# First norms of groups 2 to 7 in period 0, a token-order router, and the experts' input split on GpSimd

## The chip, the core and the metric

The kernel runs on one core of one Trainium2 chip. The metric is the device time of one execution in microseconds (us), the median of several runs. The five engines of the core each follow an instruction list of their own and meet at semaphores: TensorE (PE in the profile), VectorE (DVE), ScalarE (ACT), GpSimd (POOL), and SyncE (SP), which issues most of the transfers.

## The reference

The input `x` is (16, 64, 16, 16) in fp32: 16 images, 64 channels, 256 positions. Three blocks add to it: a graph convolution behind a group norm, a selective state-space layer behind a layer norm over the 64 channels of a token, and a mixture of eight experts, two per token, behind a second such norm.

```python
x = x + L0_conv(_gn(x), ...)
t = _to_tokens(x)                    # 16 x 256 tokens of 64 channels
t = t + L1_attn(_ln_t(t), ...)       # "first norm": x_proj = norm(t) @ W_in
t = t + L1_ffn(_ln_t(t), ...)        # "second norm": router and experts read it
# in L1_attn: a scan over time, for 128 inner channels x 16 states
h_new = exp(dt * A) * h + dt * B * x_t;   y_t = (h_new * C).sum(-1)
# in L1_ffn, xt being _ln_t(t):
logits = xt @ Wr + br;   weights of the two largest of softmax(logits)
xn = (xt - mu) * rsqrt(var + eps)    # a norm of the normed input
h = gelu((xn * ln_g + ln_b) @ W1 + b1);   y = h @ W2 + b2
```

## The kernel before, in words

Channels lie on the partitions, two images side by side (64 + 64 partitions), so a **group** is two images and there are eight, 0 to 7, each 128 x 256 numbers. The state-space layer sees a group as 128 inner channels x 512 tokens. A prepared stage does the convolution and leaves its result in `res`; then `body` runs on every engine for **periods** i = 0 to 7. In period i the scan of group i runs; the experts of group i-1 (`prev`) are worked out beside it, and the first norm, projections and step sizes of group i+2 (`nxt2`) and the broadcast transfers of group i+1 (`nxt`) are made ready. Period 0 has no experts. After period 7 comes a tail: the experts of group 7 alone.

The order on each engine is written out by hand; nothing is scheduled. Main parts of one period:

- **VectorE**: eight slots (`dve_slot`, L797), each a product into PSUM (L810) and a scan of 1024 columns (L816). After slot 0: `dve_gate` (L833, gates the last period's scan output), `dve_relu`, `dve_t1` (adds the residual). After slot 1: the second norm's products and the router. That is `dve_lnF` (L844, `tns`), four half-width products with the experts' input in `dve_xn2` (L849: `xnt2` in fp32 and `X2`'s upper half, rounded to fp32r), two router steps in between (`dve_router1`), then eleven small ones (`dve_router2`, L872) with the first norm's product for group i+2 (`dve_xn`, L819) inside. Later, four products with the experts' outputs (`dve_mes`).
- **ScalarE**: sixteen decays (`act_decay`, L602, exp of 128 x 510; blocks 8 to 15 read PSUM that TensorE fills just before, `pe_spread`), between them the squares, Ln and Exp of the two norms (`act_lnF1`, `act_lnF2`, `act_lnA1`, `act_lnA2`), one Exp for the router, 16 gelus, three table loads, and copies.
- **GpSimd**: eight products of the scans with C (`pool_slot`, L348), the step sizes of the next group (`step_input`), the low part of the experts' input (`pool_x2`, L391: fp32 minus rounded, 64 x 512), the router's last five small steps (`pool_router`, L399), sums of the expert outputs.
- **TensorE**: the spreads, the norms' centring and averaging as matrix products with `cen_m` and `avg_m`, the router's logits (`pe_router`), the experts. Each first layer is two products, with high and low weights, on `X2`, which holds the rounded input on partitions 0 to 63 and the remainder on 64 to 127. Behind four first layers `pe_wt` (L1230) transposes the token weights that `pool_router` made, then second and first layers alternate to the end. Then the projections of group i+2 and `pe_sum` (L1107), the sums over states, whose last quarter waits for GpSimd's slot 7 and releases the next `dve_gate`. `pe_warm` are products whose result nobody reads.

In period 0 ScalarE itself issues the transfers of group 1's step sizes (`step_out`, L710).

## Time and profile before

| | |
|---|---|
| median of 3 runs | 395.13 us (391.87 to 396.75) |
| profiled execution | 391.73 us, span 390.0 us |
| busy: PE, DVE | 327.2 us (84%), 322.9 us (83%) |
| busy: ACT, POOL | 277.1 us (71%), 267.6 us (69%) |
| mean granted TensorE clock | 0.948 of full speed |

Busy shares are means over a preparation of about 55 us, eight periods and a tail of 35 us. In the periods VectorE, ScalarE and TensorE are all close to full, so a share alone doesn't tell which of them ends a period; the timelines of one period do. Period i is taken from one gate on VectorE to the next. The "granted clock" is the share of TensorE's full clock that the chip let through: 1.0 is 2.4 GHz, 0.5 is 1.2 GHz.

### The profile page before, as it was taken

The page shows a single profiled execution, that of the slowest core. Times are in us where ns is not written, and L with a number is a line of the kernel's source. Part 1 is how long each engine was busy: PE and PEld are TensorE (multiplying, and loading weights), DVE is VectorE, ACT ScalarE, POOL GpSimd, SP SyncE. Part 2 cuts the span into 40 slices and gives each one's busy share as a digit, 9 for nine tenths or more (in the row PEclk, how much of TensorE's full clock was granted, in tenths as well). Part 3 has the DMA queues.
Part 4 walks back from the last instruction along what each step waited for, and adds up shares of the span by engine and source line. Part 5 has one row for each costly group of instructions (what it writes and reads, how often), then busy time and mean ns, then how long its engine had stood idle before and what let it go on. Part 6 is the DMA issues. An engine that isn't in the chain of part 4 may idle for free. (4 is left out here: it accounts for less than half of the span.)

```text
span 390.0 us, 5520 instructions
## 1 busy us (share of the span) xinstructions
PE 327.2 (84%) x1680; PEld 178.4 (46%) x1680; DVE 322.9 (83%) x428; ACT 277.1 (71%) x465; POOL 267.6 (69%) x255
## 2 busy tenths in 40 slices
PE   0597897488899889978997899799889877998894
PEld 0475445232555345434544453455245424545452
DVE  2774466997999999999999999999999989994411
ACT  1003557589988997899789979997998749661472
POOL 8804403797669967996699589958985895692132
PEclk9996999558999999999999999999999998999698
...
GB/s 192 226 109 59 2 145 229 213 221 224 208 214 225 221 194 221 182 135 230 197 181 135 226 198 195 125 213 229 180 134 212 228 162 8 2 3 13 0 2 13
DMA packets 21301, 59.54 MB, mean 153 GB/s; under 512 B 4988, under 2 KB 13336, under 8 KB 15384
## 3 DMA queue, kind: packets, MB, share of 16 engines
...
q8 instruction: 14, 0.23, 0.3%
q14 instruction: 15, 0.12, 0.1%
...
## 5 line engine op out<-in xcount | busy, mean ns | idle before, releaser
L353 POOL TENSOR_TENSOR hs<-hs,Cs 128x1024 f32<-128x1024 f32 x63 | 149.6, 2377 | 39.5 <-DVE hs L816 38.8
L816 DVE TENSOR_TENSOR_SCAN hs<-av,P 128x1024 f32<-128x1024 f32 x64 | 146.3, 2286 | 4.8 <-ACT av L617 1.5
L680 ACT ACTIVATE hb<-P,b1c 128x512 f32<-128x512 f32 x128 | 81.3, 686 | 12.2 <-PE P L1266 11.9
L810 DVE TENSOR_TENSOR P<-P,ub 128x1024 f32<-128x1024 f32 x62 | 76.0, 1225 | 2.3 <-DMA ub<-u_scratch 0.6
L1280 PE MATMUL P<-hb,W2s 128*64 128x256 f32 x512 | 69.5, 395 | 0.0
L1265 PE MATMUL P<-X,W1H 128*128 128x512 f32 x128 | 57.8, 451 | 4.2 <-ACT hb L680 3.2
L1266 PE MATMUL P<-X,W1L 128*128 128x512 f32 x128 | 52.4, 409 | 0.0
L617 ACT ACTIVATE av<-P,Aneg 128x510 f32<-128x510 f32 x68 | 43.9, 685 | 9.8 <-PE P L1209 6.2
L1280 PEld LDWEIGHTS P<-hb,W2s 128*64 128x64 f32 x512 | 31.6, 137 | 31.0 <-issue 21.2
L617 ACT ACTIVATE av<-av,Aneg 128x510 f32<-128x510 f32 x60 | 38.2, 707 | 0.1
L1209 PE MATMUL P<-D,selD 128*128 128x512 f32 x64 | 29.8, 507 | 6.8 <-ACT av L617 4.2
L1265 PEld LDWEIGHTS P<-X,W1H 128*128 128x128 f32 x128 | 24.8, 194 | 22.5 <-ACT hb L680 15.0
L1117 PE MATMUL P<-hs,selS 128*32 128x512 f32 x256 | 30.6, 598 | 3.9 <-POOL hs L353 3.9
L673 ACT ACTIVATE wbs<-P 128x512 f32<-128x512 f32 x32 | 19.1, 598 | 15.4 <-PE P L1245 15.4
L367 POOL TENSOR_TENSOR accs<-accs,mes 128x512 f32<-128x512 f32 x21 | 26.9, 1282 | 2.4 <-DVE mes L917 2.4
L1266 PEld LDWEIGHTS P<-X,W1L 128*128 128x128 f32 x128 | 25.1, 196 | 3.8 <-issue 1.0
L1209 PEld LDWEIGHTS P<-D,selD 128*128 128x128 f32 x64 | 12.3, 198 | 19.3 <-issue 18.0
L917 DVE TENSOR_TENSOR mes<-P,wbs 128x512 f32<-128x512 f32 x28 | 18.6, 666 | 0.0
L1117 PEld LDWEIGHTS P<-hs,selS 128*32 128x32 f32 x256 | 6.8, 109 | 25.9 <-POOL hs L353 13.7
L907 DVE SCALAR_TENSOR_TENSOR mes<-P,cols,wbs 128x256 f32<-128x256 f32 x8 | 3.5, 480 | 16.5 <-PE P L1280 8.8
L1296 PE MATMUL P<-W1H 128*128 128x512 f32 x53 | 16.0, 406 | 0.0
L389 POOL TENSOR_TENSOR D<-dts,D 64x512 fp32r<-64x512 f32 x8 | 10.2, 1271 | 7.8 <-ACT D L600 6.9
...
## 6 DMA issues: line engine op xcount, KB each, us to landing
...
```

The costliest lines, as they stand in the source:

```text
L353: gp.tensor_tensor(hs[:, at, :, :], hs[:, at, :, :], rep(Cs[:, p, :], 1, 2), ALU.mult).then_inc(S["cm"], 1)
L367: done = gp.tensor_tensor(acc[:, :, :], prev, mes[:, at:at + 2, :], ALU.add)
L617: a_.activation(steps, dt_of, ACT.Exp, scale=Aneg[:, m:m + 1]).then_inc(S["aexp"], 1)
L673: a_.activation(wbs[:, 2 * r:2 * r + 2, :].rearrange("p e f -> p (e f)"), P[:, YS, :], ACT.Copy).then_inc(S["wb"], 1)
L680: a_.activation(hb[:, r % 4, :], P[:, (XA, XB)[r % 2], :], ACT.Gelu, bias=b1c[:, r:r + 1]).then_inc(S["gl"], 1)
L810: v.tensor_tensor(ring, rep(P[:, BB, :], 1, 2), ub[:, 2 * n:2 * n + 2, :], ALU.mult).then_inc(S["bm"], 1)
L816: v.tensor_tensor_scan(hs[:, (SLOTS * g + n) % RING].rearrange("p a t -> p (a t)"), av[:, 2 * n:2 * n + 2, :].rearrange("p a t -> p (a t)" ...
L1117: last = pe.matmul(P[32 * q:32 * q + 32, YS, :], selS[:, k, :], hs[:, (SLOTS * g + n) % RING, q % 2, :], start=(k == 0), stop=(k == 3))
L1209: pe.matmul(P[:, (YS, XA)[m % 2], :], selD[:, m - BY_PE[0], :], D2[:, :], start=True, stop=True).then_inc(S["dt_pe"], 1)
L1265: pe.matmul(P[:, bank, :], W1H[:, e, 128 * k:128 * k + 128], X2[:, :], start=True, stop=False)
L1266: pe.matmul(P[:, bank, :], W1L[:, e, 128 * k:128 * k + 128], X2[:, :], start=False, stop=True).then_inc(S["f1"], 1)
L1280: last = pe.matmul(P[64 * h:64 * h + 64, (XC, XD)[pair % 2], HW * (e % 2):HW * (e % 2) + HW], W2s[:, e, k, :], hb[:, r % 4, HW * h:HW * h ...
```

## The change

Three things are done, and order is moved around them.

1. **First norms in period 0.** Groups 2 to 7 get their first norm in period 0 already, two groups at a time (512 columns): `pe_cenP`, `act_lnP1`, `pe_varP`, `act_lnP2`, `dve_xnp`, k = 0, 1, 2. The results stay on chip in `xnl` (128 x 6 x 256). The per-period norm of group i+2 goes from all engines in periods 0 to 5.
2. **Token-order router.** The logits are now made from `t1` itself, with router weights that were multiplied by `cen_m` once (`Wrc`). The variance is made once more with tokens on the partitions (`pe_vartok`: 128 x 4), so ScalarE's Ln and Exp for the router shrink from 128 x 256 to 128 x 4. VectorE scales 128 x 32 logits and adds the bias, in place of the product `tns` of 128 x 256. Four of the router's results go to PSUM that lay in SBUF before.
3. **Experts' input.** VectorE makes one product of 128 x 256 (`dve_xn1`) where it made four of 64 x 256. GpSimd rounds it (two casts of 64 x 256) and takes the remainder (two subtractions of 64 x 256), before its product of slot 1 from period 1 on. In period 0 slot 1 goes ahead of `step_input`.

Buffers are laid over others to make room. In the tail the experts' input is made on VectorE as before, the router's logits move ahead, and the idle products are 2, 3 and 9 where they were 2, 4, 6 and 3.

```diff
+        sq2, rqs = hb[:, 3, 0:HW], hb[:, 3, HW:T]
+        sq, rs = ygs[:, 0:HW], ygs[:, HW:T]
+        sqp = mes[:, 0:2, :].rearrange("p r t -> p (r t)")
+        rsp = mes[:, 2:4, :].rearrange("p r t -> p (r t)")
...
         def pool_x2(eng, g):
...
             eng.wait_ge(S["xn2"], 2 * (g + 1))
-            eng.wait_ge(S["xh2"], 2 * (g + 1))
-            eng.wait_ge(S["cm"], min(SLOTS * (g + 1) + 2, SLOTS * G))
-            since(eng, "acc", EXP * g)
-            gp.tensor_tensor(X2[64:128, :], xnt2[:, :], X2[0:64, :], ALU.subtract).then_inc(S["xl2"], 1)
+            since(eng, "f1", EXP * KC * g)
+            eng.wait_ge(S["u"], so_far(g, 3))
+            eng.wait_ge(S["cm"], SLOTS * (g + 1) + 1)
+            for h in range(2):
+                q = slice(64 * h, 64 * h + 64)
+                gp.tensor_copy(X2[q, HW * h:HW * h + HW], xn[q, :]).then_inc(S["xh2"], 1)
+            for h in range(2):
+                q, o = slice(64 * h, 64 * h + 64), slice(64 - 64 * h, 128 - 64 * h)
+                eng.wait_ge(S["xh2"], 2 * g + h + 1)
+                low = gp.tensor_tensor(X2[o, HW * h:HW * h + HW], xn[q, :], X2[q, HW * h:HW * h + HW], ALU.subtract)
+            low.then_inc(S["xl2"], 1)
...
+                if i == 0:
+                    pool_slot(eng, i, p, 1)
                 if nxt is not None:
                     step_input(eng, gp, nxt, q)
-                pool_slot(eng, i, p, 1)
                 if prev is not None:
                     pool_x2(eng, prev)
+                    eng.wait_ge(S["xl2"], prev + 1)
+                if i > 0:
+                    pool_slot(eng, i, p, 1)
+                if prev is not None:
                     pool_router(eng, prev)
...
+        def act_lnP1(eng, k):
+            eng.wait_ge(S["cen1"], k + 3)
+            since(eng, "var1", k + 2)
+            a_.activation(sqp, P[:, XD, :], ACT.Square).then_inc(S["sq1"], 1)
+
+        def act_lnP2(eng, k):
+            eng.wait_ge(S["var1"], k + 3)
+            eng.wait_ge(S["xn1"], 2 * k + 2)
+            a_.activation(rsp, P[:, XC, :], ACT.Ln, bias=epst[:, 0:1]).then_inc(S["ln1"], 1)
+            eng.wait_ge(S["ln1"], k + 3)
+            a_.activation(rsp, rsp, ACT.Exp, scale=-0.5).then_inc(S["rs1"], 1)
...
         def act_rs2(eng, g):
-            a_.activation(rs2[:, :], P[:, XB, HW:T], ACT.Ln, bias=epst[:, 0:1]).then_inc(S["ln2"], 1)
+            eng.wait_ge(S["vt"], g + 1)
+            a_.activation(rv[:, 6], P[:, XC, 4 * EXP:4 * EXP + 4], ACT.Ln, bias=epst[:, 0:1]).then_inc(S["ln2"], 1)
...
         def act_lnF2(eng, g):
...
+            act_rq(eng, g)
+            act_rs2(eng, g)
+            act_rq_exp(eng, g)
+            act_rs2_exp(eng, g)
...
+                if i == 0:
+                    act_lnP1(eng, 0)
                 act_decay(eng, i, *((4, 5, 6, 7) if i > 0 else (6, 7)))
                 if i == 0:
+                    act_lnP2(eng, 0)
...
@@ -716,17 +739,20 @@
...
                 act_decay(eng, i, 11)
-                if nxt2 is not None:
-                    act_lnA1(eng, nxt2)
-                act_decay(eng, i, 12, 13)
+                if i == 0:
+                    act_lnP1(eng, 1)
+                act_decay(eng, i, 12)
+                if i == 0:
+                    act_lnP2(eng, 1)
                 if prev is not None:
                     act_router(eng, prev)
-                if nxt2 is not None:
-                    act_lnA2(eng, nxt2)
+                act_decay(eng, i, 13)
...
                     act_dhi(eng, nxt)
+                    act_lnP1(eng, 2)
                     act_c(eng, nxt, q, YS)
+                    act_lnP2(eng, 2)
...
+        def dve_xnp(eng, k):
+            eng.wait_ge(S["rs1"], k + 3)
+            if k == 2:
+                eng.wait_ge(S["g_mm"], 2)
+            v.tensor_tensor(xnl[:, 2 * k:2 * k + 2, :].rearrange("p g f -> p (g f)"), P[:, XD, :], rsp, ALU.mult).then_inc(S["xn1"], 2)
...
+        def dve_xn1(eng, g):
+            eng.wait_ge(S["rq"], g + 1)
+            since(eng, "xl2", g)
+            v.tensor_tensor(xn, P[:, XB, 0:HW], rqs, ALU.mult).then_inc(S["xn2"], 2)
...
         def dve_router1(eng, g):
-            logits = P[:, XC, 0:4 * EXP].rearrange("p (c e) -> p c e", e=EXP)
-            eng.wait_ge(S["lg"], 2 * (g + 1))
+            logits = P[:, XC, 224:224 + 4 * EXP].rearrange("p (c e) -> p c e", e=EXP)
+            eng.wait_ge(S["rs2"], g + 1)
+            eng.wait_ge(S["lg"], g + 1)
+            scaled = P[:, XC, 192:192 + 4 * EXP].rearrange("p (c e) -> p c e", e=EXP)
+            v.tensor_tensor(scaled, P[:, XC, 0:4 * EXP].rearrange("p (c e) -> p c e", e=EXP), rep(rv[:, 7], 2, EXP), ALU.mult).then_inc(S["lm"], 1)
+            eng.wait_ge(S["lm"], 2 * g + 1)
+            v.tensor_tensor(logits, scaled, rep(brs[:, :], 1, 4), ALU.add).then_inc(S["lm"], 1)
+            eng.wait_ge(S["lm"], 2 * g + 2)
             v.tensor_reduce(rv[:, 0], logits, AX, ALU.max).then_inc(S["m1"], 1)
...
-            v.scalar_tensor_tensor(out=rt[:, 5], in0=rt[:, 4], scalar=-2.0, in1=chances, op0=ALU.mult, op1=ALU.add).then_inc(S["e2"], 1)
+            v.scalar_tensor_tensor(out=left, in0=rt[:, 4], scalar=-2.0, in1=chances, op0=ALU.mult, op1=ALU.add).then_inc(S["e2"], 1)
...
-            v.tensor_tensor(rt[:, 6], rt[:, 5], bc(2), ALU.is_equal).then_inc(S["s2"], 1)
+            v.tensor_tensor(second, left, bc(2), ALU.is_equal).then_inc(S["s2"], 1)
...
-            v.tensor_tensor(rt[:, 7], rt[:, 6], rank[:, :, :], ALU.mult).then_inc(S["s2r"], 1)
+            v.tensor_tensor(weighed, second, rank[:, :, :], ALU.mult).then_inc(S["s2r"], 1)
...
                 if prev is not None:
-                    dve_lnF(eng, prev)
-                    dve_xn2(eng, prev)
-                    dve_router2(eng, prev, nxt2)
+                    dve_router1(eng, prev)
+                    dve_xn1(eng, prev)
+                    dve_router2(eng, prev)
...
                 dve_slot(eng, i, 3)
+                if i == 0:
+                    dve_xnp(eng, 0)
                 dve_slot(eng, i, 4)
                 experts(0)
                 dve_slot(eng, i, 5)
                 if i == 0:
-                    dve_xn(eng, 2)
+                    dve_xnp(eng, 1)
                 experts(2)
                 dve_slot(eng, i, 6)
+                if i == 0:
+                    dve_xnp(eng, 2)
...
+        def pe_cenP(eng, k):
+            eng.wait_ge(S["xn1"], 2 * k + 2)
+            pe.matmul(P[:, XD, :], cen_m[:, :], res[:, slice(2 * (k + 1) * HW, 2 * (k + 2) * HW)], start=True, stop=True).then_inc(S["cen1"], 1)
+
+        def pe_varP(eng, k):
+            eng.wait_ge(S["sq1"], k + 3)
+            eng.wait_ge(S["sg"], 2)
+            since(eng, "ln1", k + 2)
+            pe.matmul(P[:, XC, :], avg_m[:, :], sqp, start=True, stop=True).then_inc(S["var1"], 1)
...
         def pe_router(eng, g):
             eng.wait_ge(S["t1"], g + 1)
-            pe.matmul(P[:, XC, 0:4 * EXP], ident[:, :], rep(brs[:, :], 1, 4), start=True, stop=False).then_inc(S["lgb"], 1)
-            eng.wait_ge(S["tn"], g + 1)
+            eng.wait_ge(S["wrc"], 1)
             for q in range(2):
-                pe.matmul(P[:, XC, 2 * EXP * q:2 * EXP * q + 2 * EXP], tns[:, 128 * q:128 * q + 128],
-                          Wrt[:, :, :].rearrange("p h e -> p (h e)"), start=False, stop=(q == 1)).then_inc(S["lg"], 1)
+                last = pe.matmul(P[:, XC, 2 * EXP * q:2 * EXP * q + 2 * EXP], t1[:, 2 * (g % 2), 128 * q:128 * q + 128],
+                                 Wrc[:, :, :].rearrange("p h e -> p (h e)"), start=True, stop=True)
+            last.then_inc(S["lg"], 1)
+
+        def pe_vartok(eng, g):
+            eng.wait_ge(S["sq2"], g + 1)
+            for q in range(2):
+                last = pe.matmul(P[:, XC, 4 * EXP + 2 * q:4 * EXP + 2 * q + 2], sq2[:, 128 * q:128 * q + 128],
+                                 avg_m[:, 0:128:64], start=True, stop=True)
+            last.then_inc(S["vt"], 1)
...
             pe_dtz(eng, 1)
+            pe_cenP(eng, 0)
...
+            eng.wait_ge(S["ld_dup"], 64)
+            last = pe.matmul(P[:, XB, 2 * EXP * 2:2 * EXP * 2 + 2 * EXP], cen_m[:, :], Wrt[:, :, :].rearrange("p h e -> p (h e)"), start=True, stop=True)
...
                 pe_spread(eng, i, 9)
+                if i == 0:
+                    pe_varP(eng, 0)
...
-                    eng.wait_ge(S["xn1"], so_far(prev, 3))
+                    eng.wait_ge(S["xn1"], G)
                     since(eng, "me", EXP * prev)
+                    pe_router(eng, prev)
                     pe_warm(eng, 2, XD)
                     pe_varF(eng, prev)
+                    pe_vartok(eng, prev)
                 pe_spread(eng, i, 11)
                 pe_spread(eng, i, 12)
-                if nxt2 is not None:
-                    pe_cenA(eng, nxt2)
-                if prev is not None:
-                    pe_router(eng, prev)
+                if i == 0:
+                    pe_cenP(eng, 1)
                 pe_spread(eng, i, 13)
-                if nxt2 is not None:
-                    pe_varA(eng, nxt2)
+                if i == 0:
+                    pe_varP(eng, 1)
                 pe_spread(eng, i, 14)
                 pe_spread(eng, i, 15)
                 if prev is not None:
-                    eng.wait_ge(S["xh2"], 2 * (prev + 1))
+                    eng.wait_ge(S["xn2"], 2 * (prev + 1))
                     pe_warm(eng, 2, XB)
+                if i == 0:
+                    pe_cenP(eng, 2)
                 if nxt is not None:
                     pe_c(eng, nxt)
+                if i == 0:
+                    pe_varP(eng, 2)
```

How the lists move, at the places that matter below. GpSimd, in period 2, from its product of slot 0 on (`rl`, `dts`: step sizes; `X`: the experts' input; `rt`, `vv`: the router's weights). Before:

```order
L353 TENSOR_TENSOR hs<-hs,Cs 128x1024 [waits cs,scan]
L338 TENSOR_TENSOR dts<-rl,sp 128x512 [waits dt_out,dlo,sp_relu,sp_ln]
L340 TENSOR_TENSOR rl<-dts,xc 128x512 [waits dt]
L353 TENSOR_TENSOR hs<-hs,Cs 128x1024 [waits scan]
L397 TENSOR_TENSOR X<-xnt,X 64x512 [waits cm,acc,xh2,xn2]
L403 TENSOR_TENSOR rt<-rt,rv 128x32 [waits o2,xl2]
L405 TENSOR_TENSOR rt<-rt 128x32 [waits num]
L408 TENSOR_TENSOR rt<-rt,rv 128x32 [waits rden,wt]
L412 CAST vv<-rt 128x4x8 [waits wtr,wn]
L414 TENSOR_TENSOR vv<-rt,vv 128x4x8 [waits vhi]
```

With the change:

```order
L353 TENSOR_TENSOR hs<-hs,Cs 128x1024 [waits cs,scan]
L338 TENSOR_TENSOR dts<-rl,sp 128x512 [waits dt_out,dlo,sp_relu,sp_ln]
L340 TENSOR_TENSOR rl<-dts,xc 128x512 [waits dt]
L399 CAST X<-xnt 64x256 [waits u,cm,f1,xn2]
L399 CAST X<-xnt 64x256
L403 TENSOR_TENSOR X<-xnt,X 64x256 [waits xh2] x2
L353 TENSOR_TENSOR hs<-hs,Cs 128x1024 [waits scan,xl2]
L410 TENSOR_TENSOR rt<-rt,rv 128x32 [waits o2,xl2]
L412 TENSOR_TENSOR rt<-rt 128x32 [waits num]
L415 TENSOR_TENSOR rt<-rt,rv 128x32 [waits rden,wt]
L419 CAST vv<-rt 128x4x8 [waits wtr,wn]
L421 TENSOR_TENSOR vv<-rt,vv 128x4x8 [waits vhi]
```

The experts' input takes four instructions for one and stands before the product of slot 1; the router's five steps stay behind that product.

TensorE, in period 1, from the second norm's centring on (`D`: spreads). Before:

```order
L1194 MATMUL P<-t1s,cen_m 128x256 [waits t1]
L1209 MATMUL P<-D,selD 128x512 [waits aexp,dlo]
L1296 MATMUL P<-W1H 128x512 [waits xn1]
L1296 MATMUL P<-W1H 128x512
L1198 MATMUL P<-sq2s,avg_m 128x256 [waits sq2]
L1209 MATMUL P<-D,selD 128x512 [waits aexp,dlo] x2
L1123 MATMUL P<-res,cen_m 128x256
L1224 MATMUL P<-brs,ident 128x32 [waits t1]
L1227 MATMUL P<-Wrt,tns 128x16 [waits tn]
L1227 MATMUL P<-Wrt,tns 128x16
L1209 MATMUL P<-D,selD 128x512 [waits aexp,dlo]
L1127 MATMUL P<-sq,avg_m 128x256 [waits sq1]
```

With the change:

```order
L1242 MATMUL P<-t1s,cen_m 128x256 [waits t1]
L1257 MATMUL P<-D,selD 128x512 [waits aexp,dlo]
L1274 MATMUL P<-Wrc,t1s 128x16 [waits wrc,t1,xn1]
L1274 MATMUL P<-Wrc,t1s 128x16
L1351 MATMUL P<-W1H 128x512 x2
L1246 MATMUL P<-hb,avg_m 128x256 [waits sq2]
L1281 MATMUL P<-avg_m,hb 128x2 [waits sq2]
L1281 MATMUL P<-avg_m,hb 128x2
L1257 MATMUL P<-D,selD 128x512 [waits aexp,dlo] x5
```

The logits stand ahead of the idle products and the average, two more products behind it, and the first norm's two are gone.

ScalarE, in period 0, from the decays of blocks 6 and 7 on. Before:

```order
L617 ACTIVATE av<-av,Aneg 128x2x255 x2
L245 DMA dt_scratch<-dts 16x8x512 [waits dt]
L247 DMA u_scratch<-rl 16x8x512 [waits u]
L617 ACTIVATE av<-P,Aneg 128x2x255 [waits dt_pe] x4
L550 ACTIVATE sq<-P 128x256 [waits var1,cen1]
L617 ACTIVATE av<-P,Aneg 128x2x255 [waits dt_pe] x2
L555 ACTIVATE rs<-P,epst 128x256 [waits xn1,var1]
L557 ACTIVATE rs<-rs 128x256 [waits ln1]
L617 ACTIVATE av<-P,Aneg 128x2x255 [waits dt_pe] x2
L600 ACTIVATE D<-dts 64x512 [waits dt_pe,dt]
L594 ACTIVATE Cs<-P,bbcol 128x512 [waits c_rep_mm]
```

With the change:

```order
L574 ACTIVATE mes<-P 128x512 [waits var1,cen1]
L641 ACTIVATE av<-av,Aneg 128x2x255 x2
L579 ACTIVATE mes<-P,epst 128x512 [waits xn1,var1]
L581 ACTIVATE mes<-mes 128x512 [waits ln1]
L245 DMA dt_scratch<-dts 16x8x512 [waits dt]
L247 DMA u_scratch<-rl 16x8x512 [waits u]
L641 ACTIVATE av<-P,Aneg 128x2x255 [waits dt_pe] x4
L574 ACTIVATE mes<-P 128x512 [waits var1,cen1]
L641 ACTIVATE av<-P,Aneg 128x2x255 [waits dt_pe]
L579 ACTIVATE mes<-P,epst 128x512 [waits xn1,var1]
L581 ACTIVATE mes<-mes 128x512 [waits ln1]
L641 ACTIVATE av<-P,Aneg 128x2x255 [waits dt_pe] x3
```

A square stands before those decays, an Ln and an Exp between them and the two transfers, and another square and pair around the decay of block 12. A third set follows behind block 15, around the copy of C.

## Rows read from the trace of the kernel before

**Rows 1.** timeline of VectorE: start us, us, engine line, operation, tiles [idle before <-releaser].
```profile
94.23 0.69 DVE L837 TENSOR_TENSOR ygs<-P,sg 128x512 f32<-128x512 f32 x1 [0.19 <-PE P L1117]
...
137.07 0.42 DVE L847 TENSOR_TENSOR tns<-P,rs2s 128x256 f32<-128x256 f32 x1
...
141.86 1.22 DVE L810 TENSOR_TENSOR P<-P,ub 128x1024 f32<-128x1024 f32 x1
...
319.30 0.69 DVE L837 TENSOR_TENSOR ygs<-P,sg 128x512 f32<-128x512 f32 x1 [0.25 <-PE P L1117]
```

**Rows 2.** timeline of ScalarE, period 2 and the next block 8.
```profile
133.59 1.24 ACT L617 ACTIVATE av<-P,Aneg 128x510 f32<-128x510 f32 x2
...
135.89 0.47 ACT L625 ACTIVATE rs2s<-P,epst 128x256 f32<-128x256 f32 x1 [0.22 <-PE P L1198]
...
137.24 0.68 ACT L617 ACTIVATE av<-P,Aneg 128x510 f32<-128x510 f32 x1
...
139.21 0.23 ACT L656 ACTIVATE P<-rt 128x32 f32<-128x32 f32 x1
139.33 0.50 ACT L555 ACTIVATE rs<-P,epst 128x256 f32<-128x256 f32 x1
...
170.95 1.26 ACT L617 ACTIVATE av<-P,Aneg 128x510 f32<-128x510 f32 x2
```

**Rows 3.** timeline of TensorE, period 2.
```profile
135.18 0.67 PE L1198 MATMUL P<-sq2s,avg_m 128*128 128x256 f32 x2
...
137.55 0.62 PE L1227 MATMUL P<-Wrt,tns 128*128 128x16 f32 x4 [0.66 <-DVE tns L847]
138.06 0.47 PE L1209 MATMUL P<-D,selD 128*128 128x512 f32 x1
...
140.99 1.10 PE L1181 MATMUL P<-xc,Wrep 128*128 128x512 f32 x2 [0.58 <-ACT av L617]
141.57 0.75 PE L1265 MATMUL P<-X,W1H 128*128 128x512 f32 x1
...
144.64 0.38 PE L1235 MATMUL P<-ident,vv 128*32 128x128 f32 x2
144.95 1.08 PE L1280 MATMUL P<-hb,W2s 128*64 128x256 f32 x8
```

**Rows 4.** timeline of GpSimd: the preparation, then period 2.
```profile
42.74 0.29 POOL L485 CAST b2h<-mes 128x128 fp32r<-128x128 f32 x1
...
137.34 2.37 POOL L353 TENSOR_TENSOR hs<-hs,Cs 128x1024 f32<-128x1024 f32 x1
...
142.08 0.24 POOL L403 TENSOR_TENSOR rt<-rt,rv 128x32 f32<-128x32 f32 x1 [0.86 <-DVE rt L899]
...
143.33 0.25 POOL L414 TENSOR_TENSOR vv<-rt,vv 128x32 f32<-128x32 f32 x1
```

**Rows 5.** groups by line, GpSimd (xcount | busy us, mean ns | idle before <-releaser).
```profile
L384 POOL TENSOR_TENSOR accs<-accs,mes 128x256 f32<-128x256 f32 x7 | 5.1, 731 | 7.2 <-DVE mes L907 6.6
```

**Rows 6.** timeline of VectorE, the last group's router.
```profile
363.75 0.20 DVE L878 SCALAR_TENSOR_TENSOR P<-P,rank 128x32 f32<-128x32 f32 x1 [0.27 <-ACT P L656]
...
365.55 0.19 DVE L899 TENSOR_TENSOR rt<-rt,rv 128x32 f32<-128x32 f32 x1
```

**Rows 7.** page, part 2: TensorE's granted clock, 40 slices of 9.75 us.
```profile
PEclk9996999558999999999999999999999998999698
```

**Rows 8.** timelines of ScalarE, TensorE and VectorE in period 0.
```profile
74.32 1.26 ACT L617 ACTIVATE av<-P,Aneg 128x510 f32<-128x510 f32 x2 [3.22 <-POOL rl L340]
...
81.77 2.05 PE L1181 MATMUL P<-xc,Wrep 128*128 128x512 f32 x2 [0.83 <-ACT av L617]
...
85.50 1.23 DVE L810 TENSOR_TENSOR P<-P,ub 128x1024 f32<-128x1024 f32 x1
```

**Rows 9.** windows of 2 us (busy, count; then granted clock), last period.
```profile
329.00:331.00 2.00, 2.00 (x5) 1.16 (x4) 1.93 (x4) 1.62 (x3) 1.20 (x5) 0.50 0.00 0
331.00:333.00 2.00, 2.00 (x10) 1.03 (x10) 1.97 (x2) 1.37 (x3) 0.10 (x1) 0.65 0.03 8
```

97 lines of the change are left out of this document (38 added, 59 removed).

## The prediction

> **What bounds the kernel now.** I read the timelines of one middle period on all engines, since the page's busy shares (83 to 84% for TensorE and VectorE) can't say who ends a period. VectorE first: from the gate at 94.23 to that at 319.30 lie six periods, 225.07 us, so 37.51 each, and before the gate VectorE idles only a quarter of a microsecond [rows 1]. That looks like a kernel that VectorE bounds. The second loop runs over ScalarE and TensorE and must be read too: block 8's decay starts at 133.59 and again at 170.95, 37.36 later [rows 2]. From that decay to the first second-layer product at 144.95 [rows 3] it is 11.36, and from there to the next block 8 it is 26.00. In those 26.00 lie the experts on TensorE, then table loads, silus and decays on ScalarE; the change touches none of it. So two loops of nearly one length run side by side. What shortens one alone brings nothing; what lengthens either is paid in every period. The question for each part is what it does to those 11.36 us.
>
> **VectorE.** The stretch behind slot 1 lasted from 137.07 to 141.86, 4.79 us [rows 1]. A dependent small step costs 0.225, since eight of them lie between 363.75 and 365.55 (1.80) [rows 6]. New: three steps from the scaling to the router's difference (0.68), about 0.6 until ScalarE's Exp is back, 1.80 for the rest and 0.11 to the next slot, 3.2 in all. The one product of 128 x 256 (0.42, as `tns` [rows 1]) lies under the wait for the Exp. So VectorE saves 1.6, of which 0.35 is lost again because it has to wait for the router's Exp (below): 1.25 a period. It is time that VectorE then spends waiting, unless the other loop shrinks as well.
>
> **The other loop, laid on period 2.** On TensorE the logits come ahead of the average: 0.51 (137.55 to 138.06), so the average starts at 135.69, not 135.18, and ends at 136.36 [rows 3]. The two token-variance products behind it have the logits' shape of work, again 0.51, and end under the first Ln. On ScalarE the first Ln starts at 136.40 for 135.89. Four Ln and Exp took 1.35; two of them shrink to 128 x 4, priced like the 128 x 32 Exp after which the next operation starts 0.12 later [rows 2]: 0.91. The router's Exp ends near 137.4, VectorE reaches its product 0.8 later, and the experts' input lies there at 138.67.
>
> Then GpSimd, which is free since its step sizes. A cast of 64 x 256 isn't in the trace. The nearest rows are the cast of 128 x 128 at 0.29 [rows 4] from below and the two-input operation of 128 x 256 at 0.73 [rows 5] from above; I take 0.40, near the cast. A subtraction of 64 x 256 is 0.73. The four make 2.3, so `X2` is ready at 141.0. The product of slot 1 takes 2.37 and the router 1.50 (142.08 to 143.58) [rows 4]: the weights are ready at 145.0. TensorE's transposes wait for them, at 145.05 where they started at 144.64 [rows 3]. That is the step on which I rest the forecast: the first layers may start earlier (141.05 for 141.57), ScalarE has lost four operations on the way, and TensorE two products, but all of it ends in the wait for the weights, because the router stands behind slot 1 on GpSimd. The loop becomes 37.36 + 0.41 = 37.77, 0.26 more than the period now: **1.6 us** over six periods. With casts at 0.29 it is 0.3, with 0.73 it is 5.6. If an extra product on TensorE costs nothing, 0.5 less a period; if 0.2 more each, 2.4 us more in all.
>
> The Trainium skill (GPSIMD Engine Reference, 4.1 Engine selection) says that GpSimd runs one input at roughly line rate but two inputs about half as fast as VectorE. By an estimate from that, half of the two-input row, a cast is 0.37 and this term 1.2. No run here shows a cast of this size.
>
> What moves and costs nothing: slot 1's product on GpSimd is needed only by the sums at the period's end. GpSimd leaves the router 1.4 later than it did (145.0 for 143.58) and is busy for 69% of the span, so it has some 11 us of waits in a period to make that up. `xnl` needs no transfer. Without that cover the sums would be late by the 1.4.
>
> **Last period and tail.** In the last period the same wait applies (+0.3). In the tail `X2` comes one product earlier (0.35) and the difference two steps later less that product (+0.1). I take 0 in all, with 1 either way.
>
> **Period 0.** Here operations are added that were not there: three passes of centring, square, average, Ln, Exp and product on 512 columns. A TensorE product of 128 x 512 takes 2.05 at the clock of this stretch [rows 8] and 1.10 at full clock [rows 3]; ScalarE takes 0.63 for an operation (half of 1.26 [rows 8]), VectorE 0.69 (the gate [rows 1]). A pass is a round trip: 2.05 + 0.63 + 2.05 + 1.26 + 0.69 = 6.7 us, or 4.8 at full clock. The granted clock is 0.5 in the slices from 68 to 88 us [rows 7], where TensorE waits for decays.
>
> Pass 0's average, Ln and Exp (3.3) stand before the transfers of group 1. ScalarE idled 3.22 there [rows 8], but for GpSimd's step sizes, and the average can't start until block 9 is spread; I take 1.9 of delay, bounds 0 and 3.3. So block 8 decays at 76.2 for 74.32. Four decays and block 12's spread later, near 79.0, pass 1 starts: product at 85.8. Pass 2's centring waits for that product (same bank) and for block 15's spread, 86.3; the projection of C stands between its centring and its average on TensorE (about 1.1 more); its product ends near 94.0. Slot 7 of VectorE stands behind it: its first product ends at 95.2, where it ended at 86.73 [rows 8]. All that follows, up to the gate at 94.23, moves with it: +8.4. At full clock the same chain ends at 90.0, and slot 7's first product at 91.2. From there to the gate it took 7.5 in the row (86.73 to 94.23), the last sums of TensorE among it; I let these gain 1.5, an assumption between nothing and the 1.9 that two such products gain (2.05 for 1.10). The gate then comes at 97.2, +3.0. I take **6.5**, nearer to the half-clock end, since the clock row is the one that this stretch showed, but with five more long products in it the clock may return earlier than it did.
>
> The transfers of group 1 start up to 3.3 later, and what reads them is 8.4 later; at full clock both are some 3, so I count nothing.
>
> **Sum.** The profiled execution took 391.73 (span 390.0 and 1.7 around it): 391.7 + 1.6 + 0 + 6.5 = 399.8. The median of the runs of before lies 3.4 above that execution, so a median would lie between 399.8 and 403.2. I say 401.
>
> **Rivals.**
>
> *The weights are not late* (20%). If GpSimd is 0.9 quicker than priced, the transposes follow the first layers: 141.05 + 3.07 (141.57 to 144.64 [rows 3]) = 144.12, the loop is 36.8 and VectorE's 36.3 fits under it. That is 0.7 less a period, 4 to 5 us in seven, so with period 0 between 3.0 and 6.5 the execution takes 389.7 to 394.2, the median up to 3.4 more. Against it: 0.73 a subtraction is a plain row.
>
> *VectorE was the only bound* (9%). Its 1.25 come back in seven periods (8.7), and period 0 costs 3.0: 386. For it: a quarter of a microsecond of idling. Against it: ScalarE's own 37.36.
>
> *Period 0 runs at full clock* (12%), the rest as forecast: 391.7 + 1.6 + 3.0 = 396.3, the median up to 3.4 more.
>
> *The clock falls among the experts* (9%), the other side, slower. TensorE now waits before block 13's spread, before the third first layer and some 0.9 us before the transposes. In the last period of before, after waits for the logits, a decay and the experts' input, the granted clock was 0.50 from 329 to 331 and 0.65 to 333 [rows 9]: 2 x 0.5 + 2 x 0.35 = 1.7 us. In seven periods 12: 412. It decides if the granted clock is under 1.0 there in most periods. In the middle periods of before, with shorter waits, the page shows 0.9 or more.
>
> The Trainium skill (TensorE: Matmul & The Clock Gate, Part 1) says that half clock is the default and activity lifts it, which speaks against a change that takes TensorE's work out between waits; the last period's row agrees with it.
>
> **How the numbers follow.** The forecast has 50% and its own range is 397 to 406. The range of 391 to 408 takes in the first rival's upper half, period 0 at full clock, the bounds of the casts and of period 0 and the distance to the median; it leaves out VectorE's case and the falling clock. Two per cent of the median is 7.9 us, about what a measurement of this kernel can tell from no change: faster is under 387.2, slower over 403.0. Faster: VectorE's case and a little of the first rival, 10%. Slower: the falling clock and two fifths of the forecast, 30%. Within: 60%.
>
> **What would show it.** Right: a gate-to-gate period of 37.6 to 37.9; VectorE idling over a microsecond before the router or the gate; the transposes waiting for GpSimd; the gate of period 1 between 98 and 103; VectorE waiting in period 0 for the Exp of passes 1 and 2; the cast near 0.40. Wrong: a period under 37.2, transposes without a wait, a first gate before 97, or a granted clock of 0.5 in the middle periods.

## The result, and the profile of the changed kernel

The changed kernel takes 403.42 us, the median of 4 runs (403.08 to 403.53), against 393.5 for the kernel before in 4 runs (the three of the table above and one of 391.31). The ratio is 1.0244, its 95% interval 1.0199 to 1.0289. The forecast was 401 with a range of 391 to 408.

The interval holds the 2% that the forecast took as its border, so the change is clearly slower, but whether by more than 2% these runs leave open. The profiled executions lie 11.7 us apart in span (401.7 and 390.0). Laid out from gate to gate on VectorE, with what the forecast gave to each stretch:

| stretch | before | after | difference | forecast |
|---|---|---|---|---|
| start to the first product of slot 0 | 55.51 | 56.69 | +1.2 | 0 |
| from there to the first gate (period 0) | 38.72 | 44.23 | +5.5 | +6.5 |
| period 1 | 37.36 | 38.95 | +1.6 | +0.3 |
| periods 2 to 6, sum | 187.71 | 188.29 | +0.6 | +1.3 |
| last period | 35.64 | 37.50 | +1.9 | 0 with the tail |
| tail | 35.06 | 36.04 | +1.0 | |

Nearly half of the 11.7 is period 0, and 4.5 are period 1, the last period and the tail; the five middle periods lost almost nothing. VectorE in the changed kernel: two of the waits of period 0, then the first gate, period 2 from gate to gate, and the last period's ends (the timeline, as in [rows 1]):

```profile
85.02 0.69 DVE L854 TENSOR_TENSOR xnl<-P,mes 128x512 f32<-128x512 f32 x1 [1.02 <-ACT mes L581]
...
91.85 0.69 DVE L854 TENSOR_TENSOR xnl<-P,mes 128x512 f32<-128x512 f32 x1 [2.68 <-ACT mes L581]
...
100.92 0.67 DVE L869 TENSOR_TENSOR ygs<-P,sg 128x512 f32<-128x512 f32 x1
...
139.87 0.69 DVE L869 TENSOR_TENSOR ygs<-P,sg 128x512 f32<-128x512 f32 x1 [0.19 <-PE P L1154]
...
146.39 0.20 DVE L897 TENSOR_TENSOR P<-P,rv 128x32 f32<-128x32 f32 x1 [1.13 <-ACT rv L658]
...
177.64 0.69 DVE L869 TENSOR_TENSOR ygs<-P,sg 128x512 f32<-128x512 f32 x1 [0.19 <-PE P L1154]
...
328.16 0.69 DVE L869 TENSOR_TENSOR ygs<-P,sg 128x512 f32<-128x512 f32 x1 [0.28 <-PE P L1154]
...
365.66 0.69 DVE L869 TENSOR_TENSOR ygs<-P,sg 128x512 f32<-128x512 f32 x1 [3.10 <-PE P L1154]
```

In period 0 VectorE waits 1.02 and 2.68 for the Exp of the second and third pass. In period 2 the gate waits 0.19, but VectorE now idles 1.13 ahead of the router as well: it is no longer the bound. 177.64 less 139.87 is 37.77. GpSimd, TensorE and ScalarE show what holds the period (timelines, as in [rows 4], [rows 3] and [rows 2]; the row of ScalarE is block 8's decay):

```profile
147.68 0.85 POOL L399 CAST X<-xnt 64x256 fp32r<-64x256 f32 x2 [2.56 <-DVE xnt L890]
...
148.60 1.52 POOL L403 TENSOR_TENSOR X<-xnt,X 64x256 fp32r<-64x256 f32 x2
...
150.20 2.38 POOL L353 TENSOR_TENSOR hs<-hs,Cs 128x1024 f32<-128x1024 f32 x1
...
153.78 0.25 POOL L421 TENSOR_TENSOR vv<-rt,vv 128x32 f32<-128x32 f32 x1
```

```profile
101.84 0.65 PE L1236 MATMUL P<-ygs,Wouts 128*64 128x256 f32 x4 [2.25 <-DVE ygs L869]
...
152.62 0.40 PE L1321 MATMUL P<-X,W1L 128*128 128x512 f32 x1
...
154.09 0.39 PE L1290 MATMUL P<-ident,vv 128*32 128x128 f32 x2 [1.08 <-POOL vv L421]
...
154.41 1.08 PE L1335 MATMUL P<-hb,W2s 128*64 128x256 f32 x8
...
341.48 0.39 PE L1290 MATMUL P<-ident,vv 128*32 128x128 f32 x2 [1.10 <-POOL vv L421]
...
341.81 1.96 PE L1335 MATMUL P<-hb,W2s 128*64 128x256 f32 x8
```

```profile
142.67 1.24 ACT L641 ACTIVATE av<-P,Aneg 128x510 f32<-128x510 f32 x2
```

On GpSimd two casts (0.85) and two subtractions (1.52), then the product of slot 1 (2.38), and only then the router; its last step ends at 154.03. TensorE is through with the fourth first layer soon after 152.62, waits 1.08, and transposes at 154.09. The last two rows of TensorE are the last period: the same wait, 1.10, and behind it the eight second-layer products take 1.96 where they took 1.08 in period 2. That is the clock. Windows (busy time and count of PE, weight loads, DVE, ACT and POOL, then the granted clock):

```profile
76.00:80.00 4.00, 2.10 (x4) 1.27 (x5) 3.71 (x3) 2.61 (x5) 3.48 (x2) 0.50 0.53 162
88.00:92.00 4.00, 3.44 (x12) 1.22 (x11) 1.32 (x2) 2.77 (x5) 3.34 (x2) 0.84 1.03 223
104.00:108.00 4.00, 4.00 (x15) 3.50 (x15) 2.44 (x2) 1.81 (x5) 1.97 (x2) 0.50 0.97 206
108.00:112.00 4.00, 3.27 (x6) 1.67 (x7) 2.92 (x16) 3.35 (x9) 1.87 (x4) 0.50 0.63 185
342.00:344.00 2.00, 2.00 (x9) 0.88 (x8) 1.97 (x2) 0.28 (x1) 1.74 (x1) 0.50 0.04 8
```

Half clock in much of period 0, 0.84 from 88 to 92, half clock again from 104 to 112 in period 1, behind a wait of 2.25 for the first gate (row 101.84), and from 342 to 344 in the last period. The last period of the kernel before had half clock too, but ahead of its second layer (329 to 333, [rows 9]); there the eight products took 1.08.

### The profile page after: what moved, and what is told of

Read it like the earlier page. It is cut to its first block and busy times, and to the rows that moved or that the text cites. A ratio compares the mean times of both kernels' runs of the same rounds, so it can differ in the third digit from the quotient of the medians.

```text
span 401.7 us, 5543 instructions
## 1 busy us (share of the span) xinstructions
PE 332.0 (83%) x1685; PEld 179.7 (45%) x1685; DVE 315.6 (79%) x413; ACT 274.8 (68%) x456; POOL 274.2 (68%) x276
## 5 line engine op out<-in xcount | busy, mean ns | idle before, releaser
L1335 PE MATMUL P<-hb,W2s 128*64 128x256 f32 x512 | 70.5, 399 | 0.0
L1320 PE MATMUL P<-X,W1H 128*128 128x512 f32 x128 | 56.5, 441 | 6.0 <-ACT hb L700 4.1
L1257 PE MATMUL P<-D,selD 128*128 128x512 f32 x64 | 31.1, 527 | 18.6 <-ACT av L641 17.4
L1154 PE MATMUL P<-hs,selS 128*32 128x512 f32 x256 | 29.6, 596 | 1.4 <-POOL hs L353 1.4
L399 POOL CAST X<-xnt 64x256 fp32r<-64x256 f32 x14 | 5.6, 397 | 21.0 <-DVE xnt L890 20.5
L1351 PE MATMUL P<-W1H 128*128 128x512 f32 x52 | 16.9, 432 | 0.0
```

Of the source, the lines that this page charges most:

```text
L1154: last = pe.matmul(P[32 * q:32 * q + 32, YS, :], selS[:, k, :], hs[:, (SLOTS * g + n) % RING, q % 2, :], start=(k == 0), stop=(k == 3))
L1257: pe.matmul(P[:, (YS, XA)[m % 2], :], selD[:, m - BY_PE[0], :], D2[:, :], start=True, stop=True).then_inc(S["dt_pe"], 1)
L1320: pe.matmul(P[:, bank, :], W1H[:, e, 128 * k:128 * k + 128], X2[:, :], start=True, stop=False)
L1335: last = pe.matmul(P[64 * h:64 * h + 64, (XC, XD)[pair % 2], HW * (e % 2):HW * (e % 2) + HW], W2s[:, e, k, :], hb[:, r % 4, HW * h:HW * h ...
L1351: pe.matmul(P[:, bank, :], W1H[:, 0, 0:128], W1H[:, 0:2, :].rearrange("p e f -> p (e f)"), start=True, stop=True)
```

## Experiments

Each is the changed kernel with one edit, unless it says otherwise. The kernel before ran beside them, 393.6 to 394.1.

**1. The router ahead of slot 1.**

```diff
-                if i > 0:
-                    pool_slot(eng, i, p, 1)
                 if prev is not None:
                     pool_router(eng, prev)
+                if i > 0:
+                    pool_slot(eng, i, p, 1)
```

> GpSimd makes the router's weights ahead of its product of slot 1 (2.37 us). Theory (the transposes wait for weights that stand behind slot 1, and this wait sets periods 2 to 6): the wait of 1.08 before the transposes goes, the period falls from 37.77 by about 1.06 to 36.7, over six periods 6.4, and in the last period the wait and the fallen clock behind it go too (0.3 to 1.9): 395 to 397. Rival (VectorE or another engine holds the period, the wait for the weights is beside the path): the period stays at 37.5 to 37.8 and the time within 1 us of 403.4. Rival (slot 1's product is now late and the sums wait for GpSimd): the gate waits longer, period over 37.8.

Measured: 396.0 (10 runs), 7.4 less than the change; ratio to before 1.007 (1.0027 to 1.0113). The wait for the weights is gone, but from gate to gate four of periods 2 to 6 take 37.2 to 37.8 and only period 6 takes 36.5. TensorE in period 3 (gate 176.10), and a window of it:

```profile
182.62 1.05 PE L1257 MATMUL P<-D,selD 128*128 128x512 f32 x2 [0.88 <-ACT av L641]
...
185.23 1.91 PE L1229 MATMUL P<-xc,Wrep 128*128 128x512 f32 x2
...
186.15 1.42 PE L1320 MATMUL P<-X,W1H 128*128 128x512 f32 x1
...
189.78 0.38 PE L1290 MATMUL P<-ident,vv 128*32 128x128 f32 x2
...
190.09 1.08 PE L1335 MATMUL P<-hb,W2s 128*64 128x256 f32 x8
```

```profile
184.00:188.00 4.00, 4.00 (x9) 2.43 (x9) 3.86 (x10) 2.47 (x4) 3.43 (x9) 0.57 0.88 211
```

The transposes follow the first layers without a wait. Yet the projection of C takes 1.91, and the first of the first layers 1.42 for 0.51: behind the wait of 0.88 the granted clock is 0.57. The first second-layer product comes 13.99 behind the gate, 14.54 in the change. So the wait was what held the period, and taking it away let the next limit show: the falling clock among the experts, which I had as a rival with 9%. It fell in periods 3 and 4 only (0.57 and, from 221 to 225, 0.59), and was 1.00 among the experts of periods 2, 5 and 6. Measured from one block 8 to the next, which leaves out how far the gate runs ahead of block 8 (2.1 to 2.8), periods 2 to 5 take 36.5, 37.9, 37.8 and 36.5: where the clock stayed, the expected 36.7 was reached; where it fell, it was missed by 1.1 to 1.2. In the profiled execution (397.07, 6.5 less than the change's) the middle periods give 2.4 of the gain, the last period 1.9 (35.65 for 37.50), the tail 1.2 and period 0 0.8.

**2. Idle products ahead of the transposes.**

```diff
                     pe_f1(eng, prev, 3)
+                    pe_warm(eng, 4, XD)
                     pe_wt(eng, prev)
```

> Four more idle products of 128 x 512 (0.23 each at full clock, 0.92) stand on TensorE ahead of the transposes. Theory (TensorE waits 1.08 there for GpSimd's weights): they fit into the wait, periods 2 to 6 stay at 37.77; period 1 had no wait there and takes 0.9 more; in the last period TensorE no longer idles before the transposes, the granted clock stays at 1.0 behind them, and the 1.6 that the half clock cost there come back: about 402.7. Rival (TensorE's own work sets the period): 0.9 more in each of seven periods, 409 to 410. Rival (the clock of the last period does not depend on that wait): the second-layer products behind the transposes stay near 1.96 and the time is 404.

Measured: 402.24. Periods 2 to 5 stay at 37.75 to 37.82 with 0.9 us more work on TensorE in each:

```profile
153.00 1.07 PE L1351 MATMUL P<-W1H 128*128 128x512 f32 x4
...
154.26 0.39 PE L1290 MATMUL P<-ident,vv 128*32 128x128 f32 x2 [0.19 <-POOL vv L421]
...
154.58 1.08 PE L1335 MATMUL P<-hb,W2s 128*64 128x256 f32 x8
```

The four products fill the wait down to 0.19, and the transposes start where they did. TensorE's own work doesn't set the period; GpSimd's weights do. The part on the clock went otherwise: in the last period (36.53) it fell ahead of the first layers (0.63 to 0.80 each) and had returned behind them (second layer 1.08). Period 1, where 0.9 more was expected, took 37.03, 1.9 less than in the change, at full clock and behind a wait of 1.01 for the gate, while period 0 took 45.75, 1.5 more; so that the total came out as expected is in part luck.

**3. The third pass's product behind slot 7.**

```diff
-                if i == 0:
-                    dve_xnp(eng, 2)
                 experts(4)
                 dve_slot(eng, i, 7)
+                if i == 0:
+                    dve_xnp(eng, 2)
```

> VectorE's product of the third pass stands behind slot 7 instead of ahead of it. Theory (in period 0 VectorE's slot 7 stands behind the round trip of the third pass and waits 2.68 for its Exp): the gate of period 1 comes 2.0 to 2.7 earlier, 400.7 to 401.4. Rival (TensorE and ScalarE carry the chain of period 0 whatever VectorE does): the gate moves by less than 0.7 and the time stays at 403.

Measured: 400.15. Period 0 fell by 0.7 only (43.56 for 44.23), so the rival has it; the rest of the gain came where the edit did not aim: in period 1 (38.21, at full clock), the last period (35.87) and the tail (35.01). VectorE and TensorE at the end of period 0:

```profile
98.77 2.29 DVE L842 TENSOR_TENSOR_SCAN hs<-av,P 128x1024 f32<-128x1024 f32 x1 [2.58 <-ACT av L641]
```

```profile
96.18 1.10 PE L1213 MATMUL P<-xc,Wdts 128*128 128x512 f32 x2 [1.76 <-ACT sg L600]
...
101.92 0.65 PE L1236 MATMUL P<-ygs,Wouts 128*64 128x256 f32 x4 [1.07 <-DVE ygs L869]
```

VectorE no longer waits for the third pass, but the scan of period 1's slot 0, the last operation ahead of the gate, now waits 2.58 for a decay of ScalarE. TensorE waits 1.76 for ScalarE's silu, which stands behind the third pass's Ln and Exp, before it can make the step sizes and the sums. The chain runs over ScalarE and TensorE, which is read from these rows; no run moved the silu. (In this execution the second pass also came 1.0 later, 29.32 behind the first slot for 28.33, so the edit may be worth up to 1.7.)

**4. Passes 1 and 2 left out.** `act_lnP1`, `act_lnP2`, `pe_cenP` and `pe_varP` are not called for k = 1, 2 (the removed calls are not shown here), and the product waits for pass 0:

```diff
...
-            eng.wait_ge(S["rs1"], k + 3)
+            eng.wait_ge(S["rs1"], 3)
```

> Passes 1 and 2 of the first norms are left out on TensorE and ScalarE; VectorE writes the product of pass 0 three times, so groups 4 to 7 get the norms of groups 2 and 3 (this part of the result is changed). Theory (the round trips of passes 1 and 2 carry most of what period 0 grew, 5.5 of it from the first slot to the gate): the gate comes 3.0 to 4.5 earlier, so 399 to 400, and what stays is pass 0's 1.3 ahead of the step-size transfers and two products of 0.69. Rival (the later transfers of group 1 or slot 1's place in GpSimd's order hold period 0): the gate moves by less than 1, 402.5 or more.

Measured: 398.69, 4.7 less. Period 0 takes 40.56, 3.7 less than with three passes and 1.8 more than before. So two thirds of what period 0 grew are the round trips of passes 1 and 2. Of the 1.8 left, 1.4 are there at block 8's decay already, behind pass 0 (20.25 behind the first product of slot 0, where it was 18.81); the rest I put down to the three products, which no run tests. GpSimd's new order in period 0 costs nothing: slot 1 fits into its wait, and the step sizes start 15.54 behind slot 0 in the change (72.23) as before (71.05).

**5. Idle products ahead of the first gate.**

```diff
                     pe_sum(eng, i, k)
+                if i == 0:
+                    pe_warm(eng, 6, XB)
```

> Six idle products on TensorE behind the sums of period 0, where it waits 2.25 for the first gate. Theory (period 1 took 38.95, 1.2 more than the others, because after that wait the granted clock fell and TensorE ran at half clock from 103 to 113): the clock stays at 1.0, period 1 falls to 37.4 to 37.8, the time to 402. Rival (period 1 is long for another reason, such as late transfers or GpSimd): no change, 403.4.

Measured: 399.19, 4.2 less where 1.4 was expected, and the expected place gives 1.4 (period 1 at 37.53):

```profile
104.00:108.00 4.00, 3.02 (x17) 2.16 (x16) 3.62 (x8) 3.44 (x11) 1.30 (x2) 1.00 0.94 210
108.00:112.00 4.00, 3.40 (x11) 1.67 (x11) 3.76 (x13) 3.88 (x6) 3.73 (x5) 1.00 0.69 211
340.00:342.00 2.00, 2.00 (x14) 1.03 (x12) 1.97 (x2) 0.69 (x2) 1.74 (x1) 1.00 0.04 8
```

The clock is 1.00 where it was 0.50. All the profiles agree on this place: behind a wait of 2.25 or 2.28 for the first gate it fell (the change, experiments 1, 6, 7, 8 and 10; in 6 and 10 for some 3 us, in the others for 10 or more), behind 1.01 to 1.07 it did not (before, experiments 2, 3, 4 and 11). What the edit did not aim at changed too: the last period took 35.87 and the tail 35.06, although the transposes of the last period wait 1.09 here as well. Behind the same wait the clock fell in the change's execution and stayed in this one, and in those of experiments 3 and 4 (35.87 and 35.92). Why is open.

**6. The router first, and three idle products ahead of block 13's spread** (with the edit of experiment 1):

```diff
                 if i == 0:
                     pe_cenP(eng, 1)
+                else:
+                    pe_warm(eng, 3, XD)
                 pe_spread(eng, i, 13)
```

> As the kernel with the router ahead of slot 1, and three idle products of 128 x 512 ahead of block 13's spread, where TensorE waits 0.88 for a decay in every period. Theory (once the weights are not late, a granted clock of 0.5 behind that wait holds the period at 37.2 to 37.8, and only the period in which it stayed at 1.0 took 36.5): periods 2 to 6 take 36.4 to 36.7, and the time falls by 2.5 to 4 from 396.0, to 392 to 393.5. Rival (VectorE holds the period at 37.2): no change, 396. Rival (the idle products delay the spread): 0.2 to 0.7 more in each period, 397 to 400.

Measured: 393.35 (10 runs), 2.7 less than experiment 1; ratio to before 0.9986 (0.9949 to 1.0023). Periods 2 to 6 take 36.46 to 36.60. TensorE in period 3 (gate 175.87), and a window of it:

```profile
182.37 1.04 PE L1257 MATMUL P<-D,selD 128*128 128x512 f32 x2 [0.18 <-ACT av L641]
...
184.48 1.02 PE L1229 MATMUL P<-xc,Wrep 128*128 128x512 f32 x2
...
185.46 0.50 PE L1320 MATMUL P<-X,W1H 128*128 128x512 f32 x1
...
188.43 1.08 PE L1335 MATMUL P<-hb,W2s 128*64 128x256 f32 x8
```

```profile
184.00:188.00 4.00, 3.68 (x13) 1.93 (x12) 3.90 (x9) 3.85 (x6) 3.51 (x8) 1.00 0.91 218
```

The same places as in experiment 1, at full clock: 1.02 for 1.91 and 0.50 for 1.42. The second layer starts 12.56 behind the gate. Three products more, and periods 2 to 5 are 0.6 to 1.2 shorter; period 6, which had kept its clock in experiment 1, stays at 36.5.

**7. Idle products in period 0.**

```diff
                     pe_varP(eng, 0)
+                    eng.wait_ge(S["b1c"], 1)
+                    eng.wait_ge(S["wrc"], 1)
+                    pe_warm(eng, 8, XB)
...
                 pe_spread(eng, i, 14)
+                if i == 0:
+                    pe_warm(eng, 6, XB)
```

> Idle products of 128 x 512 in period 0: eight behind pass 0's average, where TensorE waits 2.9, and six behind block 14's spread, where it waits 1.9. Theory (period 0's chain runs at half clock because TensorE stands idle there): the granted clock from 80 to 92 is 0.9 or more, passes 1 and 2 are quicker by 1 to 3, the gate comes that much earlier, 400.5 to 402.5. Rival (the clock is not to be lifted by that, the products only add work at half clock, 0.43 each): the spreads wait for them, the gate 0.5 to 2 later, 404 to 405.5.

Measured: 396.4 (10 runs, 395.54 to 402.25), 7.0 less, where 1 to 3 were expected. The profiled execution was the longest of these, 402.25 (slot 0 began at 58.48, and period 1 ran at half clock again), so only its period 0 is read here, 41.51 for 44.23:

```profile
80.00:84.00 4.00, 3.25 (x10) 1.54 (x10) 3.93 (x3) 2.43 (x5) 3.21 (x2) 1.00 0.73 183
84.00:88.00 4.00, 3.51 (x11) 1.61 (x9) 3.96 (x4) 3.85 (x7) 2.79 (x2) 1.00 1.04 225
```

With full clock from 78 on period 0 costs 2.8 more than before it did (38.72), with the change's clock 5.5. These 2.7 are the part of the gain that a trace shows. The mean granted clock of the other nine executions was 0.964 to 0.970, of the profiled one 0.938; where in them the rest was gained no trace shows.

**8. The split of the experts' input undone.** VectorE makes four half-width products (`dve_xn2`), GpSimd one subtraction behind slot 1:

```diff
...
-                if prev is not None:
-                    pool_x2(eng, prev)
-                    eng.wait_ge(S["xl2"], prev + 1)
                 if i > 0:
                     pool_slot(eng, i, p, 1)
                 if prev is not None:
+                    pool_x2(eng, prev)
                     pool_router(eng, prev)
...
-                    dve_xn1(eng, prev)
+                    dve_xn2(eng, prev)
...
```

> The third part alone undone: VectorE makes the experts' input in four half-width products again, GpSimd takes the remainder in one subtraction (1.27) behind slot 1, and the router follows it. Theory (the split is what puts the weights behind slot 1 and the casts): the remainder is there at the same time as now, the weights 1.3 earlier, so TensorE no longer waits for them; VectorE works 1.3 more, its own sum is about 37.0, and that is the period in place of 37.77: 398.5 to 400. Rival (VectorE is the bound and the split saves it): the period grows by about 1, 410. Rival (the weights are not what sets the period): no change, 403.4.

Measured: 402.03. The middle periods take 37.4, not 37.77, so the weights were the limit; but not 37.0 either. VectorE and TensorE in period 3:

```profile
178.49 0.69 DVE L860 TENSOR_TENSOR ygs<-P,sg 128x512 f32<-128x512 f32 x1 [0.25 <-PE P L1145]
...
184.14 0.20 DVE L888 TENSOR_TENSOR P<-P,rv 128x32 f32<-128x32 f32 x1 [0.25 <-ACT rv L649]
...
215.89 0.69 DVE L860 TENSOR_TENSOR ygs<-P,sg 128x512 f32<-128x512 f32 x1 [0.26 <-PE P L1145]
```

```profile
190.83 0.38 PE L1281 MATMUL P<-ident,vv 128*32 128x128 f32 x2
...
191.14 1.08 PE L1326 MATMUL P<-hb,W2s 128*64 128x256 f32 x8
```

The second layer starts 12.65 behind the gate, with no wait ahead of the transposes, and from there to the next block 8 it is 26.6, not 26.0, so this loop has room. VectorE idles 0.25 twice, so 36.9 of the 37.4 are its own: it is the nearest to a bound, though no run here takes work from it alone. The expected total was missed mainly because the middle periods fell by 0.4 each and not by 0.8; period 1 (39.50) and the tail (36.73) were longer than in the change as well.

**9. What helped, together.** Experiments 1, 3, 5, 6 and 7, and six idle products in the tail ahead of the third first layer.

```diff
...
             pe_pair(eng, G - 1, 0)
+            pe_warm(eng, 6)
             pe_f1(eng, G - 1, 2)
```

> All that helped, together: the router ahead of slot 1, three idle products ahead of block 13's spread, idle products in period 0 (eight and six) and six ahead of the first gate, the third pass's product behind slot 7, and six idle products in the tail where TensorE waits 1.96 for the third gelu. Theory (the losses are separate waits and fallen clocks, and add up): from the 393.4 of the kernel with the router first and three idle products, 2.7 less in period 0, 1.0 less in period 1, 0.7 to 1.7 less for the third pass, 0.7 less in the tail: 387 to 389, below the kernel before. Rival (the clock falls elsewhere instead): 391 to 394.

Measured: 388.66 (386.93 to 389.7, 6 runs); ratio to before 0.9856 (0.9822 to 0.989). The page's clock and VectorE's gates:

```profile
PEclk9997999899999999999999999999999999999999
```

```profile
96.46 0.66 DVE L869 TENSOR_TENSOR ygs<-P,sg 128x512 f32<-128x512 f32 x1
...
134.12 0.69 DVE L869 TENSOR_TENSOR ygs<-P,sg 128x512 f32<-128x512 f32 x1 [0.27 <-PE P L1154]
...
170.62 0.69 DVE L869 TENSOR_TENSOR ygs<-P,sg 128x512 f32<-128x512 f32 x1 [0.27 <-PE P L1154]
```

A version that beats both kernels, the one before by 1.4%. Periods 2 to 6 are 36.5 to 36.6, period 0 is 40.37, the tail 33.91. Period 1 still takes 37.66, at full clock: the six products ahead of the gate end after it and put the output projection 0.5 late (1.39 behind the gate, in the change 0.92). Whether that is all of it no run shows.

**10. Three of the router's results back in SBUF** (on top of experiment 6). These three are all that the change moved; the fourth, `ranked`, lay in PSUM before it too.

```diff
-            ranked, left, second, weighed = (P[:, XC, k:k + 4 * EXP].rearrange("p (c e) -> p c e", e=EXP) for k in (128, 256, 288, 320))
+            ranked = P[:, XC, 128:128 + 4 * EXP].rearrange("p (c e) -> p c e", e=EXP)
+            left, second, weighed = rt[:, 5], rt[:, 6], rt[:, 7]
```

> As the kernel with the router first and three idle products (393.4), but three results of the router (left, second, weighed) lie in SBUF again. Theory (an operation of VectorE with two operands in SBUF lasts until GpSimd's running instruction ends: in the kernel before the comparison of 128 x 32 took 0.42 while GpSimd worked and 0.19 in the tail): the comparison takes 0.4 to 0.9 for 0.20 in every middle period, the weights come 0.2 to 0.6 later, period 36.6 to 37.0, 394 to 396.5. Rival (the place of these results costs nothing): rows of 0.20 and 393.4.

Measured: 396.84, 3.5 more than experiment 6 and 0.3 above what was expected; periods 2 to 6 take 36.95 to 37.04. VectorE and GpSimd in period 3:

```profile
184.77 0.63 DVE L923 TENSOR_TENSOR rt<-rt,rv 128x32 f32<-128x32 f32 x1
...
185.43 0.75 DVE L926 TENSOR_TENSOR rt<-rt,rank 128x32 f32<-128x32 f32 x1
```

```profile
184.61 1.52 POOL L403 TENSOR_TENSOR X<-xnt,X 64x256 fp32r<-64x256 f32 x2
...
186.79 0.24 POOL L410 TENSOR_TENSOR rt<-rt,rv 128x32 f32<-128x32 f32 x1 [0.67 <-DVE rt L932]
```

Two operations with both operands in SBUF take 0.63 and 0.75 for 0.20: the first ends at 185.40, when the first of GpSimd's two subtractions does (184.61 and half of 1.52), the second at 186.18, right behind the end of both (186.13). GpSimd then waits 0.67 for the router's last step. This part of the change is worth 0.44 a period once the weights are on the path.

**11. The kernel before with idle products in period 0.** 

```diff
                 pe_spread(eng, i, 9)
+                if i == 0:
+                    eng.wait_ge(S["b1c"], 1)
+                    pe_warm(eng, 8, XB)
```

> The kernel before with eight idle products in its own period 0, where TensorE waits 3.3 for the decay of block 8. Theory (period 0 is long for its half clock, there too): the granted clock from 76 to 88 rises, the gate comes 1 to 2 earlier, 392. Rival (before, VectorE carries period 0, and the clock is beside the path): no change, 393.6.

Measured: 393.62, ratio 1.0003 (0.9972 to 1.0035). The clock rose (1.00 from 76 to 80, 0.84 from 84 to 88, where it was 0.50), and period 0 stayed at 38.78 for 38.72. There VectorE carries most of it: in both executions it works without a wait from slot 3 to the end of slot 7 (70.2 to 89.0 before). So idle products shorten period 0 (experiment 7) only where the added passes had put TensorE on the path.

## Why the prediction was right, and which step was short

**The two loops.** Right, in the mechanism and in its terms. From block 8's decay (142.67) to the first second-layer product (154.41) it is 11.74 in the changed kernel, forecast 11.77; from there to the next block 8 (180.43) 26.02, forecast 26.00. The weights behind slot 1 hold periods 2 to 5 at 37.77, the number forecast. Experiment 2 shows it by filling the wait, experiment 1 by removing it. VectorE's saving turned into 1.13 of idling, where over a microsecond was forecast; with the split undone (experiment 8) the period is 37.4 again. The sum of these periods grew by 0.6 for 1.3, because period 6, in which no later group is made ready, took 37.20 (37.45 before) with the same wait in it; why is not traced.

**The prices.** The cast took 0.397 (14 of them, 5.6 us), forecast 0.40; the subtraction 0.729, forecast 0.73; the four took 2.44 for 2.3. The estimate of 0.37 from the Trainium skill (GPSIMD Engine Reference, 4.1 Engine selection) was nearly as good: two inputs took 1.8 times what one did.

**Period 0.** Right in kind, a little over in size: 5.5 for 6.5. The forecast's times must be read from the first product of slot 0, since the preparation ended 1.2 later; that the gate came at 100.92, where 94.23 and the forecast's 6.5 make 100.7, is luck. Block 8 decayed 1.3 later than before (1.9 forecast). The second pass's product ended 29.0 behind slot 0 (30.3 forecast), the third's 35.9 (38.5 forecast). In each of these passes only the first TensorE product ran at half clock: the centrings took 1.91, the averages 1.13 and 1.02. From the end of slot 7's first product to the gate little was gained (7.2 for 7.5), where 1.5 was assumed at full clock. At full clock the forecast was 3.0; experiment 7 gives 2.8. The order of the chain had one step short: behind the third pass it runs over ScalarE's silu and TensorE as well as over VectorE, so that freeing VectorE gained 0.7 and not 2 (experiment 3).

**The step that was short: "I take 0 in all" for the last period and the tail,** and with it the rule that a wait costs its own length. In the last period the wait cost what was forecast (gate to first second-layer product 13.65 for 13.38, 0.27), but the clock fell behind it, and the products that followed took 1.6 more; experiments 3, 4 and 5, with the same wait and the clock at 1.00, took 35.87 to 35.92. In the tail the second layer began 0.12 later (0.1 forecast). Half clock lasted 6.8 us there, as long as before, but it began 2.2 later, in a wait of 1.96 for the third gelu, and so still held for the first layers behind the first eight second-layer products, which took 1.96 for 1.14: 1.0 in all. Period 1 lost 1.6 (a wait of 2.25 for the gate), of which experiment 5 gave back 1.4. Together some 4 us in the profiled execution. I had the falling clock as a rival only in the form "in all seven periods", 412; it came in three places. The Trainium skill (TensorE: Matmul & The Clock Gate, Part 1) has half clock as the default that activity lifts; experiments 5, 6 and 7, which only add activity, agree.

**The preparation** grew by 1.2, without a term. It is no part of the change that I can name: over 13 profiles of these kernels slot 0 began at 55.5 to 58.5, and the profile of before has the earliest.

**The sum.** For the profiled execution the forecast was 399.8; 403.53 is 3.7 more: 1.2 of preparation, 1.3 in period 1 and 2.9 in the last period and the tail, less 1.0 in period 0 and 0.7 in the middle periods. So part of the nearness is errors that cancel. The 1.2 that the forecast added for a median did not come either: the four runs of the change lie within 0.5. At a ratio of 1.0244 the change is slower by about the 2% that divides the cases; 60% stood on "within" and 30% on "slower".
